# One group's routing count on VectorE: fifteen instructions in a PSUM bank behind iteration 204, or seven parts in SBUF behind iterations 204 to 210

## The reference

```
x  = x + L0_attn(xn) * silu(L0_ffn(xn))      # softmax attention, 16 heads, 2 x 1024 tokens; mixture of 8 experts, top 2
xn = layernorm(x)
x  = x + L1_attn(xn) * silu(L1_ffn(xn))      # recurrence; mixture of 8 experts, top 2:
    scores = softmax(xf @ gate_w.T)
    _, sel = top_k(scores + expert_bias, 2)
    counts = zeros(8).at[sel_flat].add(1)    # how many rows each expert gets
    order  = argsort(sel_flat)               # rows sorted by expert
    ...
```

## Time and profile before

| | us |
|---|---|
| median of 3 runs | 1004.33 |
| lowest and highest run | 1002.76, 1007.37 |
| span of the profiled execution | 1003.7 |
| TensorE busy in the span | 920.3 |
| VectorE busy in the span | 764.0 |
| GpSimd busy in the span | 597.9 |

### The profile page before, as it was taken

How to read it: one execution, slowest core, us unless ns; L and a number is a source line. 1 busy time by engine, 2 the same in 40 slices (tenths; PEclk the granted TensorE clock), 3 DMA queues, 4 the chain that set the end, 5 groups by cost and what they waited for, 6 DMA issues and landing times. The chain is left out here.

```text
span 1003.7 us, 20954 instructions
## 1 busy us (share of the span) xinstructions
PE 920.3 (92%) x7704; PEld 489.4 (49%) x7713; DVE 764.0 (76%) x1332; ACT 538.3 (54%) x901; POOL 597.9 (60%) x533
## 2 busy tenths in 40 slices
PE   5799997999999999999989997899889787799997
PEld 3346563233333333333323233798788444488794
DVE  6978888888888889887888825883689998873514
ACT  1255345666766666666756775443266243274463
POOL 3660425788778777887777893123735886652333
PEclk9999998999999999999999999799999997999999
DMA  9372525111111101111101123567651200243462
GB/s 319 137 225 88 153 64 156 41 51 46 26 52 28 58 24 49 34 55 56 35 26 44 40 67 116 161 193 241 225 156 35 89 22 22 79 142 101 143 196 79
DMA packets 92308, 97.17 MB, mean 97 GB/s; under 512 B 23184, under 2 KB 68624, under 8 KB 91952
## 3 DMA queue, kind: packets, MB, share of 16 engines
q1 hardware_dynamic: 87088, 85.34, 27.8%
q0 software_dynamic: 5120, 10.50, 3.6%
HBM read 70.57 MB, written 24.77 MB: 95 GB/s over the span
## 5 line engine op out<-in xcount | busy, mean ns | idle before, releaser
L255 PE MATMUL ps<-ar 64*64 64x512 bf16 (+5 forms) x5312 | 538.6, 448 | 17.7 <-ACT ar L301 4.3
L255 PEld LDWEIGHTS ps<-ar 64*64 64x64 bf16 (+2 forms) x5312 | 268.5, 137 | 273.4 <-ACT ar L301 92.0
L277 DVE TENSOR_REDUCE small<-ps 128x2 f32<-128x1024 f32 (+2 forms) x276 | 307.2, 1140 | 52.0 <-PE ps L255 50.6
L301 ACT ACTIVATE ar<-ps 128x1024 f32<-128x1024 f32 (+1 forms) x304 | 285.4, 941 | 113.1 <-PE ps L255 106.5
L264 POOL TENSOR_TENSOR psum_sb<-psum_sb,ar 128x1024 f32<-128x1024 f32 x91 | 214.8, 2360 | 57.3 <-DVE on_sb L264 47.1
L264 POOL TENSOR_TENSOR ar<-ar 128x512 f32<-128x512 f32 (+1 forms) x80 | 79.2, 995 | 52.1 <-DVE ar L277 30.0
L323 POOL DMA_INDIRECT gT<-ysort,rt x48 | 46.9, 977 | 98.7 <-issue 97.7
L264 DVE TENSOR_TENSOR ar<-ps,ar 128x256 f32<-128x256 f32 (+4 forms) x56 | 56.2, 1011 | 47.9 <-PE ps L255 43.4
L264 POOL TENSOR_TENSOR psum_sb<-ar 128x1024 f32<-128x1024 f32 x32 | 75.9, 2372 | 16.8 <-ACT ar L301 15.6
L298 ACT COPY ar<-ps 128x256 f32<-128x256 f32 (+1 forms) x84 | 31.8, 386 | 80.8 <-PE ps L255 50.2
L255 PE MATMUL ps<-wA,xnT 128*128 128x512 f32 (+3 forms) x192 | 62.0, 447 | 5.3 <-DVE ar L264 2.7
(11 more groups left out here) (156 smaller groups left out, 1066.0 us busy)
## 6 DMA issues: line engine op xcount, KB each, us to landing
ar<-in_L_up SPq DMA_DIRECT2D x48, 384.0 KB, 4.1
ar<-in_L_b SPq DMA_DIRECT2D x32, 322.0 KB, 3.4
rec_sb<-lscr SPq DMA_DIRECT2D x64, 128.0 KB
scr<-ar SPq DMA_DIRECT2D x48, 128.0 KB, 2.1
ar<-xsort SPq DMA_DIRECT2D x40, 128.0 KB
ysort<-ar SPq DMA_DIRECT2D x40, 128.0 KB, 3.3
ar<-scr SPq DMA_DIRECT2D x32, 112.0 KB
xsort<-xs SPq DMA_DIRECT2D x12, 256.0 KB, 6.2
```

Of the source, the lines that this page charges most:

```text
L255: return self.e.matmul(o, l, r, start=start, stop=stop) if self.e else Nothing()
L277: return self.e.tensor_reduce(o, a, AX.X, op, negate=True) if negate else self.e.tensor_reduce(o, a, AX.X, op)
L301: return self.e.activation(o, a, fn, **kw) if self.e else Nothing()
```

## The change

Three things change, for group 2 alone. First, the intermediate results lie in SBUF (`counting`, 512 columns of the big array `ar`, where one buffer of the attention's queries is no longer used) and no longer in the bank: a copy of the ranks is added, and the first scan reads the bank and writes SBUF. Behind that scan the bank is emptied. Second, `counted` is a generator of seven parts. Third, the table places one part behind each of the iterations 204 to 210; before, all stood behind 204. Other groups run the same instructions in one piece as before.

```diff
@@ SIDE_B, vector
-204 end0.1 route.2 207 route.2 ln.1.1 208 route.2 route.2 210 route.2 214
+204 end0.1 route.2 205 route.2 206 route.2 207 route.2 ln.1.1 208 route.2 209 route.2 210 route.2 214
@@
+    counting = area(20480, 512)
@@ counted(q)
             def pcol(o, k):
-                return ps[:, bank["ranks", q], o:o + k]
+                return counting[:, o:o + k] if q == 2 else ps[:, bank["ranks", q], o:o + k]
...
             dve.wait_ge(*at("ranks", q))
-            done(dve.scan(incl, C("seg16" if n == 16 else "seg8"), pcol(128, 8 * n), 0.0, ALU.mult, ALU.add))
+            p = ps[:, bank["ranks", q], :]
+            if q == 2:
+                dve.wait_ge(*at("st", 191))
+                dve.cp(row, p[:, 0:8 * n]).then_inc(*up((t,)))
+            ins = dve.scan(incl, C("seg16" if n == 16 else "seg8"), p[:, 128:128 + 8 * n], 0.0, ALU.mult, ALU.add)
+            if q == 2:
+                ins.then_inc(*emptied(("ranks", q), ("ranks_read", q)))
+                dve.wait_ge(*at("ranks_read", q))
+                dve.wait_ge(*last(t))
+            else:
+                done(ins)
+            yield
             done(dve.tt(v3(cmp8, 8), incl[...]..., C("steps")..., ALU.is_gt))
             done(dve.red(cs, v3(cmp8, 8), ALU.add))
+            yield
             dve.scan(cums, cs, C("w8"), ...)
             done(dve.scan(cumsp, cs, C("w8"), ...))
             done(dve.tt(bases, cums, cs, ALU.subtract))
+            yield
             done(dve.stt(by_expert(Rs[:, 0:8 * n]), bases..., float(HALF), by_expert(row), ALU.mult, ALU.add))
+            yield
             done(dve.tt(row, Rs[:, 0:8 * n], incl, ALU.add))
             done(dve.tt(row, row, oh, ALU.mult))
+            yield
             done(dve.red(sls, ..., ALU.add))
             done(dve.cp(slots[q][:, 0:n], sls), "slots")
+            yield
             ...
             dve.ts(experts[q][:, 0:nt], ejs, ..., ALU.min, ALU.mult).then_inc(
-                *emptied(("ranks", q), ("experts", q)))
+                *(up((t,), ("experts", q)) if q == 2 else emptied(("ranks", q), ("experts", q))))
@@ route_beside(q)
-            counted(q)
+            yield from counted(q)
```

More of the change, by code:

```diff
@@ L122 @@
     "vector": (
[7 rows of a table removed]
+        "-1 gather.1 29 gather.1 34 gather.1 gather.1 40 gather.1 64 gather.1 72 gather.1 104 gather.1 111 gather.1 127 gather.1 133 end0.0 137 end0.0 138 end0.0 139 gather.1 140 ln.1.0 144 end0.1 154 end0.1 156 end0.1 158 ln.1.1 165 ln.1.0 166 end0.0 175 route.2 176 route.2 route.2 177 route.2 route.2 182 route.2 183 ln.1.0 184 route.2 189 route.2 190 route.2 194 route.2 199 route.2 route.2 202 route.2 route.2 ln.1.1 204 end0.1 route.2 205 route.2 206 route.2 207 route.2 ln.1.1 208 route.2 209 route.2 210 route.2 214 ln.1.1 216 route.2 217 route.2 route.2 route.2 route.2 218 route.2 221 route.2 225 route.2 227 route.2 route.2 230 route.2 238 route.2 242 route.2 route.2 ln.1.0 247 route.2 255 route.2 "),
     "scalar": (
@@ L1670, in route_alone @@
             yield
-            counted(q)
+            for _ in counted(q):
+                pass
             if layer == 0:
```

## The result

The changed kernel takes 1007.02 us (median of 20 runs, 1004.57 to 1013.69) beside 1002.86 for the kernel before (20 runs, 999.57 to 1007.62). The ratio is 1.0042 with an interval of 1.0026 to 1.0058, so 2.6 to 5.8 us slower. The ratio lies inside the 0.5% (5.0 us) that the prediction called no change; the interval lies wholly on the slower side and its upper end is a little beyond that limit. The profiled execution has a span of 1008.1 and a time of its own of 1009.85, which is 2.8 above the median. I predicted 1008.6, which is 4.3 us above the 1004.33 that I had for the kernel before; measured are 4.2 us above 1002.86.

The account below looks back on a forecast made before the run. TensorE was taken to bound the loop. VectorE's waits for GpSimd put `on_sb` 3.1 us later and part 7 adds 1.2: +4.3 on 1004.33 gives 1008.6 us, range 1000.9 to 1011.2.

Parts of the forecast that it names:

- The bank's wait goes: TensorE's 2.62 us wait for bank 2 before `st` 206 disappears; `st` 206 starts at 524.40.
- The place in SBUF costs nothing by itself: Counting instructions moved from bank to SBUF: 229 ns against 233 for 128x64, so costed at nothing.
- VectorE waits for additions: A VectorE instruction with two SBUF inputs waits for GpSimd's running addition to end, up to 2.36 us.
- the slack takes it all: Rival: no or short waits on GpSimd, VectorE's slack absorbs the spread parts; gain 3.8 us, 1000.5; chance 0.14.
- Part 2 and `st` 208: Behind reduction 205, part 2 waits for an addition and ends at 527.5; `st` 208 starts after 1.8 us idle.
- the difference waits for a semaphore, and the next addition starts first: In part 3, behind the scans, the difference is held until 532.15; TensorE idles 3.4 us before `st` 209.
- VectorE wins the gaps: Rival: part 3's difference slips in before the third addition; `on_sb` +1.5, with part 7 +2.7, 1007.0; chance 0.22.
- my own chain: Main forecast, the step-by-step waits of the parts behind 205 to 210: +4.3 us, 1007.4 to 1009.8; chance 0.44.
- 1.7 us lost to the clock again: hidden behind VectorE: From `st` 209 on, TensorE loses 1.7 us to a lower clock, but VectorE's lateness covers it.
- the clock isn't hidden: Rival: two TensorE idle spans, 1.8 and 3.4 us, cost a second uncovered 1.7 us: +6.0, 1010.3; chance 0.17.
- 1.8 us of slack: Behind `on_sb` of 210, `st` 213 can absorb 1.8 us of reduction 211's 3.0 us lateness, leaving 1.2 us.
- +3.1 and +1.2: The two summed losses: `on_sb` of 210 comes 3.1 us later, part 7 behind it adds 1.2 us.

Follow-up runs that it names:

- the tiny additions: Changed kernel with GpSimd's eight additions of units 25 and 26 cut from 1024 columns to 8: 995.4 us in one run.
- the probes: Kernel before with one extra small VectorE instruction on SBUF operands, three kinds in turn, behind steps 3, 4 and 6 of units 7 to 15: 1016.81 us.
- all behind 204: Changed kernel with all seven parts placed behind iteration 204, results still in SBUF: 1013.02 us.
- pair behind 218: Changed kernel with part 7's last two instructions, the `tensor_scalar` pair, moved behind iteration 218: median 1006.13 us, ratio to the kernel before 1.0003.
- the last experiment: Kernel before with only the last four counting instructions in SBUF, behind `on_sb` of 210 and 218: median 1000.02 us, ratio to the kernel before 0.9957.

## Why the prediction was right in its total and wrong in two steps

- **The bank's wait goes.** Right, as the row of 48 matmuls shows.
- **The place in SBUF costs nothing by itself.** Right: 3.22 us beside 3.31 for the fourteen instructions.
- **VectorE waits for additions.** Right, and shown by the tiny additions (no wait above bare durations, 6.8 us gone) and by the probes. The rival *the slack takes it all* is what the tiny additions gave, and only they gave it.
- **Part 2 and `st` 208.** Predicted to end at 527.5 with 1.8 us idle behind it; measured 527.55 (a small reduction follows at 527.33) and 1.72.
- **The step that failed first: "the difference waits for a semaphore, and the next addition starts first".** The second scan ended at 529.80 and the difference ran from 529.84 in 0.17 us. The record of the third addition starts at 529.84 too; it lasts 2.38 us, hardly longer than the others (2.34 and 2.36), and the difference is not held. I had called a gap of 0.1 us too short for a semaphore, but the semaphore costs 0.04 us here, and in the kernel before it was 0.03 (scan ended 524.14, difference at 524.17). I had named "if the difference in part 3 gets in first" as what makes the prediction fall, and "the unit between the two `on_sb` at 21 to 23 us" as a sign of being right: the first came, and the unit took 19.92. So the idle time before `st` 209 was 0.97 and not 3.4, and what came was the rival *VectorE wins the gaps*, with part 5 waiting to 535.40 (I had put that at 535.4 for this rival) and `on_sb` 1.17 us late (+1.5 there). I had 0.22 on it and 0.44 on my own chain. What I had not put into either is that part 4 waits too: 1.19 us in place of 0.3, and 0.88 us of idle time ahead of the projection behind it.
- **The clock.** I carried "1.7 us lost to the clock again: hidden behind VectorE". Nothing was lost: all windows of this stretch stand at 1.00. The rival *the clock isn't hidden* is out, though its idle span of 3.4 us never came.
- **The step that failed second: "1.8 us of slack" ahead of `st` 213.** That the pair waits was right, and so was the reduction of 211 being late, 2.6 us (it starts 3.18 behind `on_sb`, and 0.6 without a part ahead of it; I had 3.0). But I took the exponential at 542.57 of the earlier trace rows for that of iteration 213. ScalarE's timeline of the kernel before shows what the excerpt of the earlier trace rows left out between 533.05 (209) and there:

```profile
537.33 2.16 ACT L301 ACTIVATE ar<-ps 128x1024 f32<-128x1024 f32 x2
...
539.97 1.01 ACT L301 ACTIVATE ar<-ps 128x1024 f32<-128x1024 f32 x1
541.24 1.02 ACT L301 ACTIVATE ar<-ps 128x1024 f32<-128x1024 f32 x1 [0.26 <-PE ps L255]
```

  The first row is 210 and 211 in one, then come 212 and 213; 542.57 and 543.86 belong to 214 and 215. The label of the earlier trace rows is wrong in the same way. `st` 213 starts 541.24 - 0.47 - 538.53 = 2.2 us behind `on_sb`, and the reduction of 211 ends 1.8 behind it: 0.4 us of slack, so 2.6 - 0.4 = 2.2 us lost. The unit grew by 2.16, and moving the pair away gave 1.79 of it back.
- **The sum.** +3.1 and +1.2 were predicted, +1.17 and +2.16 came: 4.3 beside 3.33. The errors (-1.9 and +1.0) have opposite signs and cancel by half. I also let "the whole amount" arrive at the end, and only 2.64 us are left at the loop's end. That the medians then differ by 4.2, so near to 4.3, is luck: 1.5 us of it are not traced to the change. With the slack counted rightly, the rival would have come to 1.5 + 2.2 = 3.7 us, 1008.0.

What stays open is the stretch behind the loop. The span of after is 4.4 us longer, of which 0.14 lies ahead of unit 202 and 2.64 in the loop. The remaining 1.6 us stand behind the loop, where TensorE's granted clock was 0.94 over 373.6 us in after and 0.97 over the same stretch before. Neither instructions nor order differ there. The same stretch, from the last `on_sb` to the end, takes 378.7 us in after and 377.1 before, but 377.3 and 375.5 in the two other kernels with the chain in SBUF (all behind 204, pair behind 218), and 372.0 to 376.9 in the remaining four. That speaks for scatter between executions, and no run isolates it; the interval from 20 runs, 2.6 to 5.8 us, holds 2.6 as well as 4.2.

## What to carry to other kernels

Before moving a chain of VectorE instructions from PSUM to SBUF, look at what GpSimd runs beside it: here the instructions of the chain in the bank took 0.16 to 0.42 us inside running additions, and a 128x128 one that took 0.29 there took up to 2.44 with SBUF operands. An instruction that has to be in SBUF goes right behind the VectorE instruction that releases GpSimd, or to where GpSimd stands still, and nothing that stands in front of an urgent reduction may meet a running addition. When slack is read from a timeline, count the instances through from a known one: one iteration's error here was worth 1.4 us.

## What the runs showed of the hardware that was not expected

- A `tensor_scalar` with one small SBUF input (128x24) waits for GpSimd's addition like an instruction with two inputs: 1.42 to 1.45 us for 0.17.
- GpSimd waits for VectorE in the same way. In the kernel before, its 128x16 conversion at 552.14 lasted 0.59 us in place of 0.20 beside `on_sb` (551.99, two SBUF inputs, 0.68 us), and in the last experiment its 128x16 addition at 550.70 took 0.66 in place of 0.22 beside `on_sb` at 550.60. The two engines hold each other up here with no semaphore between them, so that engines "meet only at semaphores" is too narrow.
- The instructions behind such a wait aren't always held again at once: scan and difference passed in 0.15 and 0.17 us around the start of the next addition, the difference behind a semaphore; in the chain in one piece the instruction after the difference then waited 2.32, and the one after that 2.44 with nothing let in between.
- Idle time and the granted clock go together loosely. Behind 2.62 us of idle time the clock was 0.66 over 5 us in the kernel before; in the changed kernel 1.72, 0.97, 0.88 and 2.83 us of idle time left it at 1.00, as 1.51 did in the last experiment. With 9.69 us it fell while TensorE still stood idle (0.60 from 528 to 531 us, mean 0.80 over the unit). What decides between these is open; no run here separates it.
